# Linear attention values brought back to rows by transposes, in a bank of their own

## The chip, the cores and the metric

The kernel runs on one core of one Trainium2 chip. The metric is device time in microseconds (us) of one execution. Names of engines: PE is TensorE, DVE is VectorE, ACT is ScalarE, POOL is GpSimd, SP is SyncE.

## The reference

One transformer block on x of 4 batches x 1024 tokens x 256 channels. The output is x plus an attention part plus a mixture-of-experts part, both of the layer-normed x. The change is in the attention part, whose core is

```
sq, sk = elu(q)+1, elu(k)+1                      # 16 heads of 16 channels
# causal linear attention, chunk by chunk, S and z carried along
num = einsum(scores*mask, v) + einsum(sq, S);  den = scores.sum + einsum(sq, z)
local  = num / clip(den, EPS)
# memory of 4 banks per head: fine outputs weighted by w, and a coarse one (banks summed)
w      = softmax(mean over tokens of n_f)        # one weight per bank, head and batch
memory = exp_prob*out_fine + (1-exp_prob)*out_coarse
output = (gate*memory + (1-gate)*local) @ w_o.T
```

## The kernel before

Three phases follow one another: tokens, experts, and attention, which takes about the second half of the time. Only `attention_phase` and the list that orders it, `attention_order`, are touched.

The attention phase walks over 4 batches x 8 tiles of 128 tokens, 32 tiles in all. One list, `ATT_ORDER`, names the steps; every engine walks the same list and does the steps that are its own, in that order, so a step that waits on an engine holds back all that stands behind it on that engine. Engines meet by semaphores (`since(engine, signal, count)` waits). Nothing is planned by cost.

PE writes into a ring of 7 PSUM banks (`a_ring`). Every step that needs a bank takes the next one in the order of the list, and first waits (`use_bank`) until the step that had it 7 uses before has been read. The banks of a tile are taken in this order: four for `scores`, then `outT`, `coarseT`, `keys`, one projection for later tiles (`keys_side`: a q, k or v step), `oproj`, `hidden`, four for `norms`, zero to three further projection steps or `xT` steps, two for `values`, `gate`, `local`. So the projection of `keys_side` takes the bank of the first `scores` step, and waits for DVE's first `probs` product of the tile.

The steps which the change and the prediction touch, per tile t (0 to 7) of batch b:

- `scores` (PE L1417, DVE L1681): products of keys and queries into four banks. DVE multiplies each by the causal mask into `probs`, four products of 256 columns.
- `values` (PE L1452, ACT L1574): `probs` times v, transposed: 32 partitions per head, of which 17 (16 values and the denominator, `HE`) are used. ACT copies them to `valT`.
- `local` (PE L1463 and L1474, DVE L1687 to L1690): PE adds up, in one bank, the state's part (`sq` times `state`, L1463) and the tile's own values, brought back from `valT` to rows of tokens by matmuls with the picked columns of an identity (L1474, four matmuls of 68 columns, which the trace shows as eight passes). DVE then makes `den`, its reciprocal, and one product of 256 columns into `local`, which is a part of `mem_rows`.
- `state` and `fold` (PE L1497, DVE L1712): the two halves of a tile are added to the running state in the bank `a_sums`, and DVE copies it out under a mask of heads, 272 columns.
- `mean`, `mexp`, `weights`: once in a batch, at t = 0, the softmax over the memory banks: DVE L1644 to L1648, ACT's exponential L1526, DVE L1654 to L1661.
- `norms` (PE L1398, ACT L1554, DVE L1669 to L1674), `coef`, `rest`, `fine`, `oproj`: the memory part and the output projection, partly one or two tiles late. POOL adds up the `fine` products (L1769 to L1774).
- `rows` on ACT (L1533) scales the gathered expert rows for POOL.

The tile's end in the list is, in the kernel before:

```
order += ahead + [("values", b, t, 0), ("values", b, t, 1)] + behind + [("gate", b, t, 0)]
...
order.append(("local", b, t, 0))
```

## Time and profile before

| | |
|---|---|
| three runs | 708.75, 712.3, 714.91 us (median 712.3) |
| the profiled execution | 708.62 us, span 706.7 us |
| busy in the span | PE 89%, DVE 72%, ACT 50%, POOL 44% |
| busy in 465 to 475 us, an ordinary stretch of attention | PE 10.00, DVE 8.44, ACT 5.40, POOL 6.25 of 10 us |

The profiled execution takes 1.9 us more than its span. It lies at the lower end of the runs, 3.7 us under the median. In attention PE is shown busy almost without a break and DVE nearly so; an engine's busy time counts a matmul up to its modelled end, so PE at 10 of 10 us is not PE at its peak.

### The profile page before, as it was taken

The page shows a single profiled execution, that of the slowest core. Times are in us where ns is not written, and L with a number is a line of the kernel's source. Part 1 is how long each engine was busy: PE and PEld are TensorE (multiplying, and loading weights), DVE is VectorE, ACT ScalarE, POOL GpSimd, SP SyncE. Part 2 cuts the span into 40 slices and gives each one's busy share as a digit, 9 for nine tenths or more (in the row PEclk, how much of TensorE's full clock was granted, in tenths as well). Part 3 has the DMA queues.
Part 4 walks back from the last instruction along what each step waited for, and adds up shares of the span by engine and source line. Part 5 has one row for each costly group of instructions (what it writes and reads, how often), then busy time and mean ns, then how long its engine had stood idle before and what let it go on. Part 6 is the DMA issues. An engine that isn't in the chain of part 4 may idle for free. (4 is left out here: it accounts for less than half of the span.)

```text
span 706.7 us, 22451 instructions
## 1 busy us (share of the span) xinstructions
PE 626.9 (89%) x7874; PEld 520.5 (74%) x7874; DVE 509.9 (72%) x1362; ACT 355.9 (50%) x902; POOL 313.4 (44%) x406
## 2 busy tenths in 40 slices
PE   1997869699499999999968999989998999989885
PEld 0785748578399999999956777777776777777663
DVE  3674829358466666666656988889888788888886
ACT  4453625252434444444435766556565475646542
POOL 1153543707481000000030766656675566666775
PEclk9999989989599999999978999999999999999996
DMA  8128271534353333333350012221140202103120
GB/s 283 64 91 277 78 257 56 189 136 149 121 167 116 117 120 118 121 114 117 116 183 34 18 33 92 84 85 32 36 137 29 84 25 65 60 17 92 33 63 32
DMA packets 60123, 71.39 MB, mean 101 GB/s; under 512 B 7612, under 2 KB 55068, under 8 KB 60028
## 3 DMA queue, kind: packets, MB, share of 16 engines
q1 hardware_dynamic: 50956, 52.61, 22.9%
q0 software_dynamic: 6656, 16.86, 7.3%
q8 instruction: 67, 1.10, 0.7%
q10 hardware_dynamic: 2416, 0.59, 0.4%
q14 instruction: 28, 0.23, 0.1%
HBM read 38.45 MB, written 31.59 MB: 99 GB/s over the span
## 5 line engine op out<-in xcount | busy, mean ns | idle before, releaser
L1741 POOL TENSOR_TENSOR tick_a<-lane 128x1 f32<-128x1 f32 x32 | 6.3, 196 | 148.1 <-POOLq L834 145.8
L1744 POOL DMA_INDIRECT yg<-d_grouped_y,from_row x64 | 62.5, 977 | 15.5 <-issue 11.6
L978 ACT ACTIVATE hb<-e_h 88x256 fp32r<-88x256 f32 x72 | 27.5, 382 | 52.7 <-PE e_h L953 52.7
L87 PE MATMUL e_up<-wb,xb 128*128 x144 | 53.0, 368 | 0.5 <-issue 0.5
L1554 ACT ACTIVATE with_mem<-a_ring 128x340 f32<-128x340 f32 x128 | 47.0, 450 | 7.8 <-PE a_ring L1398 7.5
L1010 DVE TENSOR_TENSOR h_sb<-e_up,silu 128x176 f32<-128x176 f32 x72 | 24.6, 342 | 35.3 <-ACT silu L973 35.3
L87 PE MATMUL e_y<-wd,hb 88*128 x146 | 48.7, 334 | 1.0 <-DVE hb L1017 1.0
L1769 POOL TENSOR_TENSOR mem_rows<-mem_rows 128x512 f32<-128x512 f32 x16 | 24.3, 1518 | 54.5 <-DVE mem_rows L1721 54.5
L1681 DVE TENSOR_TENSOR probs<-a_ring,causal 128x256 f32<-128x256 f32 x128 | 45.1, 415 | 3.5 <-remote 3.3
L89 PE MATMUL e_up<-wb,xb 128*128 x144 | 46.9, 326 | 0.0
L88 PE MATMUL e_up<-wb,xb 128*128 x144 | 46.9, 326 | 0.0
L973 ACT ACTIVATE silu<-e_up 128x176 f32<-128x176 f32 x72 | 22.9, 318 | 41.1 <-PE e_up L89 41.1
L1474 PE MATMUL a_ring<-ident,valT 128*128 128x68 f32 x256 | 35.3, 279 | 8.4 <-ACT valT L1574 8.4
L88 PE MATMUL e_y<-wd,hb 88*128 x146 | 41.6, 285 | 0.0
L1474 PEld LDWEIGHTS a_ring<-ident,valT 128*128 128x128 f32 x256 | 31.0, 191 | 14.2 <-issue 11.0
L89 PE MATMUL e_y<-wd,hb 88*128 x146 | 41.3, 283 | 0.0
L1017 DVE TENSOR_TENSOR hb<-e_h,hb 88x256 fp32r<-88x256 f32 x72 | 30.3, 420 | 14.7 <-ACT hb L978 12.5
L821 POOL DMA_INDIRECT d_rows<-v,slot_i x32 | 34.0, 1063 | 9.5 <-issue 9.5
L821 POOL DMA_INDIRECT d_rows<-sqT,slot_i x32 | 33.0, 1032 | 9.5 <-issue 9.5
L1430 PE MATMUL a_ring<-wo,attT 128*128 128x256 f32 x128 | 35.2, 399 | 1.3 <-ACT attT L1563 1.1
L1571 ACT ACTIVATE hid<-a_ring,b 64x128 f32<-64x128 f32 x32 | 11.6, 364 | 48.6 <-PE a_ring L1440 36.8
L87 PE MATMUL t_g<-xT,shared_w 128*128 128x512 f32 (+1 forms) x48 | 22.1, 461 | 15.6 <-issue 15.6
(300 smaller groups left out, 2069.7 us busy)
## 6 DMA issues: line engine op xcount, KB each, us to landing
xg<-d_rows SPq DMA_DIRECT2D x77, 128.0 KB, 2.0
d_grouped_y<-y_sb SPq DMA_DIRECT2D x73, 128.0 KB, 1.8
d_base<-xn_in SPq DMA_DIRECT2D x8, 512.0 KB
xn_in<-d_xn SPq DMA_DIRECT2D x4, 1024.0 KB
total<-d_base SPq DMA_DIRECT2D x8, 512.0 KB
out<-total SPq DMA_DIRECT2D x7, 512.0 KB, 3.3
mem_rows<-in_w_up SPq DMA_DIRECT2D x4, 704.0 KB
v<-in_x_tok SPq DMA_DIRECT2D x2, 1024.0 KB
```

Of the source, the lines that this page charges most:

```text
L87: pe.matmul(out, a[0], b[0], start=start, stop=False)
L88: pe.matmul(out, a[0], b[1], start=False, stop=False)
L89: return pe.matmul(out, a[1], b[0], start=False, stop=stop)
L821: pool.indirect_dma_start(d["rows"], bass.IndirectOffsetOnAxis(ap=slot_i[u][:, k, t:t + 1], axis=0), xn[u][:, t, :], None).then_inc(s_sc[u ...
L978: act.activation(hb[o][0][:, :, :], ps_h[o][0:FC, 0:2 * P].rearrange("p (k n) -> p k n", k=2), ACT.Copy).then_inc(s_hh, 1)
L1010: dve.tensor_tensor(h_sb[q][:, :], ps_up[q][:, F:2 * F], silu[q][:, :], ALU.mult).then_inc(s_h, 1)
L1017: dve.tensor_tensor(hb[o][1][:, :, :], ps_h[o][0:FC, 0:2 * P].rearrange("p (k n) -> p k n", k=2), hb[o][0][:, :, :].bitcast(F32), ALU.subt ...
L1430: mm = pe.matmul(ps[:, 0:H], attT[t % 2][:, m, :], c["wo"][:, m, :], start=(m == 0), stop=(m == KC - 1))
L1474: mm = pe.matmul(ps[:, 0:NH * HE].rearrange("p (m g n) -> p m g n", m=KC, g=PP)[:, :, g, :], valT[:, g, :], pick.rearrange("p (m r) e -> p ...
L1554: act.activation(with_mem[((b - 1) * NT + t) % 3][:, j:NP:PP, :], ps[:, 0:KC * WN].rearrange("p (m w) -> p m w", m=KC), ACT.Copy).then_inc ...
L1681: dve.tensor_tensor(probs[:, j, :, :], ps[:, 0:4 * CH].rearrange("p (h i) -> p h i", i=CH), c["causal"][:, 0:CH].unsqueeze(1).broadcast_to ...
L1744: pool.indirect_dma_start(yg[tile % GATHERS][:, k, :], None, d["grouped_y"], bass.IndirectOffsetOnAxis(ap=c["from"][:, k, tile:tile + 1], ...
```

## The change

1. `local` on PE is only the state's part, in a bank of its own, the heads in another order (by_group). ACT copies it to `so_far` (272 columns).
2. A new step `picks`: PE transposes `valT` by four transposes of 128x128 into another bank. DVE adds `so_far` to it into `heads` (272 columns; in the first tile of a batch, half of the partitions are copied and half are added), and makes `den`, reciprocal and product from `heads`; the product is two of 128 columns, since the heads are in another order.
3. The exponential `mexp` on ACT comes after `gate` instead of ahead of `values`, and DVE's `weights` in the next tile, behind the `scores` products, instead of ahead of the second `fold`.

```
@@ attention_order
+        if t == 1:
+            order.append(("weights", b, 0, 0))
         if i:
             order += [("coef", *tiles[i - 1], 0), ("rest", *tiles[i - 1], 0)]
...
         if t == 0:
-            order += [("mean", b, 0, 0), ("mexp", b, 0, 0)]
+            order.append(("mean", b, 0, 0))
         order += ahead + [("values", b, t, 0), ("values", b, t, 1)] + behind + [("gate", b, t, 0)]
+        if t == 0:
+            order.append(("mexp", b, 0, 0))
...
-        if t == 0:
-            order.append(("weights", b, 0, 0))
...
-        order.append(("local", b, t, 0))
+        order += [("local", b, t, 0), ("picks", b, t, 0)]
@@ PE, local
+                        by_group = ps[:, 0:NH * HE].rearrange("p (g m n) -> p m g n", g=PP, m=KC)
...
-                               state[(2 * t + h) % 3][:, m, :],
-                               start=(first and m == 0), stop=last, skip_group_check=last)
+                               state[(2 * t + h) % 3][:, m, :].rearrange("p (g n) -> p g n", g=PP),
+                               start=(m == 0), stop=True, skip_group_check=True)
+                    elif what == "picks":
                         since(pe, s_valT, b * 2 * NT + 2 * (t + 1))
                         for g in range(4):
-                            mm = pe.matmul(ps[:, 0:NH * HE].rearrange("p (m g n) -> p m g n", m=KC, g=PP)[:, :, g, :],
-                                           valT[:, g, :], pick.rearrange("p (m r) e -> p m r e", m=KC),
-                                           start=(t == 0 and g == 0), stop=(g == 3))
+                            mm = pe.transpose(ps[:, g * P:(g + 1) * P], valT[:, g, :], c["ident"][:, :])
@@ ACT
+                    elif what == "local":
+                        since(act, s_both, b * NT + t)
+                        of = slice(0 if t else CH, P)
+                        act.activation(so_far[of, :, :], ps[of, 0:NH * HE].rearrange("p (h e) -> p h e", e=HE),
+                                       ACT.Copy).then_inc(s_before, 1)
@@ DVE
-                        link(dve.scalar_tensor_tensor(den[:, :], heads[:, :, HD], EPS, over_keep[:, :],
-                                                      ALU.max, ALU.mult))
+                        since(dve, s_before, b * NT + t + 1)
+                        since(dve, ready["picks"], b * NT + t + 1)
+                        if t:
+                            link(dve.tensor_tensor(heads[:, :, :], inside, so_far[:, :, :], ALU.add))
+                        else:
+                            dve.tensor_copy(heads[0:CH, :, :], inside[0:CH])
+                            link(dve.tensor_tensor(heads[CH:P, :, :], inside[CH:P], so_far[CH:P, :, :], ALU.add))
+                        dve.sem_inc(s_both, 1)
+                        link(dve.scalar_tensor_tensor(den[:, :], heads[:, :, HD], EPS, over_keep[:, :], ALU.max, ALU.mult))
                         link(dve.reciprocal(den[:, :], den[:, :]))
-                        dve.tensor_tensor(local[:, :].rearrange("p (h e) -> p h e", e=HD), heads[:, :, 0:HD],
-                                          den[:, :].unsqueeze(2).broadcast_to([P, NH, HD]),
-                                          ALU.mult).then_inc(s_local, 1)
+                        for m in range(KC):
+                            ins = dve.tensor_tensor(
+                                local[:, m * P:(m + 1) * P].rearrange("p (g r e) -> p g r e", g=PP, r=2),
+...
+                        ins.then_inc(s_local, 1)
```

The order of PE's instructions around the step, for tile 3 of a batch. Before, from the state's part on:

```order
L1463 MATMUL a_ring<-state,sqT 64x136
L1474 MATMUL a_ring<-ident,valT 128x2x34 [waits a_valT]
L1474 MATMUL a_ring<-ident,valT 128x2x34 x3
...
L1406 MATMUL a_ring<-ident,skT 128x128 [waits a_sk,a_local]
L1406 MATMUL a_ring<-ident,skT 128x128
L87 MATMUL a_ring<-a_xT,wqkv 128x512 [waits a_xl,a_probs]
```

and with the change:

```order
L1470 MATMUL a_ring<-state,sqT 64x4x34
L1477 MATMUL a_ring<-ident,valT 128x128 [waits a_valT,a_with]
L1477 MATMUL a_ring<-ident,valT 128x128 x3
...
L1410 MATMUL a_ring<-ident,skT 128x128 [waits a_sk,a_both]
L1410 MATMUL a_ring<-ident,skT 128x128
L87 MATMUL a_ring<-a_xT,wqkv 128x512 [waits a_xl,a_probs]
```

The transposes stand where the matmuls stood, `keys` (the transposes of skT) now waits for DVE's addition and no longer for its product, and the projection behind it (L87) still waits for `probs`. On DVE, the end of the first tile of a batch and the beginning of the second, before:

```order
L1648 TENSOR_TENSOR mw<-mw,mw_m 128x64 [waits a_dve]
L1654 TENSOR_REDUCE mw_m<-mw 128x16 [waits a_mexp]
L1655 RECIPROCAL mw_m<-mw_m 128x16 [waits a_dve]
L1656 TENSOR_TENSOR mw_m<-mw_m,half_gate 128x16 [waits a_dve]
L1658 TENSOR_TENSOR mw<-mw,mw_m 128x64 [waits a_dve]
L1661 TENSOR_TENSOR mw<-mw,alive 128x64 [waits a_dve]
L1712 TENSOR_TENSOR state<-a_sums,same_head 128x272 [waits a_ps_state,a_dve]
L1687 SCALAR_TENSOR_TENSOR den<-a_ring,over_keep 128x16 [waits a_ps_local]
L1689 RECIPROCAL den<-den 128x16 [waits a_dve]
L1690 TENSOR_TENSOR mem_rows<-a_ring,den 128x256 [waits a_dve]
L1681 TENSOR_TENSOR probs<-a_ring,causal 128x256 [waits a_ps_values,a_ps_scores] x4
```

and with the change:

```order
L1655 TENSOR_TENSOR mw<-mw,mw_m 128x64 [waits a_dve]
L1730 TENSOR_TENSOR state<-a_sums,same_head 128x272 [waits a_ps_state]
L1699 COPY heads<-a_ring 64x272 [waits a_ps_picks,a_before]
L1700 TENSOR_TENSOR heads<-a_ring,so_far 64x272
L1702 SCALAR_TENSOR_TENSOR den<-heads,over_keep 128x16 [waits a_dve]
L1703 RECIPROCAL den<-den 128x16 [waits a_dve]
L1705 TENSOR_TENSOR mem_rows<-heads,den 128x128 [waits a_dve]
L1705 TENSOR_TENSOR mem_rows<-heads,den 128x128
L1689 TENSOR_TENSOR probs<-a_ring,causal 128x256 [waits a_ps_values,a_ps_scores] x4
L1662 TENSOR_REDUCE mw_m<-mw 128x16 [waits a_mexp]
L1663 RECIPROCAL mw_m<-mw_m 128x16 [waits a_dve]
```

The five instructions of `weights` have moved from ahead of the second `fold` to behind the four `probs` products, and what stands between `fold` and `probs` has grown from three instructions to six (five in the other tiles). On ACT, at the end of the same tile, before:

```order
L1526 ACTIVATE mw<-mw 128x64 [waits a_mx]
L1574 ACTIVATE valT<-a_ring 128x4x64 [waits a_ps_local,a_ps_values] x2
L1550 ACTIVATE v<-a_ring 128x16x16 [waits a_ps_v]
L1578 ACTIVATE e_t<-a_ring,half_b 128x1 [waits a_rest,a_ps_gate]
L1533 ACTIVATE yg<-yg,cw 128x256 [waits a_ga1]
```

and with the change:

```order
L1573 ACTIVATE valT<-a_ring 128x4x64 [waits a_ps_picks,a_ps_values] x2
L1549 ACTIVATE v<-a_ring 128x16x16 [waits a_ps_v]
L1582 ACTIVATE e_t<-a_ring,half_b 128x1 [waits a_rest,a_ps_gate]
L1525 ACTIVATE mw<-mw 128x64 [waits a_mx]
L1578 ACTIVATE so_far<-a_ring 64x272 [waits a_both,a_ps_local]
L1532 ACTIVATE yg<-yg,cw 128x256 [waits a_ga1]
```

The copies to `valT` no longer stand behind the exponential; the new copy `so_far` does.

## Rows read from the trace of the kernel before

**Rows 1.** The page: busy time of the engines, and the chain that ended last.

```profile
PE 626.9 (89%) x7874; PEld 520.5 (74%) x7874; DVE 509.9 (72%) x1362; ACT 355.9 (50%) x902; POOL 313.4 (44%) x406
...
PE 28%; DVE 9%; issue 4%; POOL 3%; ACT 3%; another core or an unknown queue 1%; ACTq 0%; POOLq 0%; DVEq 0%
```

**Rows 2.** Waits, 375 to 706 us: waiter, waited for, us, times, longest.

```profile
DVE den L1687 <- PE a_ring L1474: 9.6, 13, 1.1
...
DVE total L1729 <- PE a_ring L1430: 4.5, 12, 1.4
DVE state L1712 <- PE a_sums L1497: 4.2, 12, 0.5
...
DVE den L1687 <- PE a_ring L1463: 2.7, 4, 0.7
```

**Rows 3.** Timeline of an ordinary tile: start, duration, instruction [idle before].

```profile
412.81 1.11 PE L1474 MATMUL a_ring<-ident,valT 128*128 128x68 f32 x8
412.82 0.62 ACT L1547 ACTIVATE sqT<-a_ring 128x512 f32<-128x512 f32 x1
...
413.85 0.69 PE L1417 MATMUL a_ring<-masked,skT 32*64 32x128 f32 x32
413.95 0.17 DVE L1687 SCALAR_TENSOR_TENSOR den<-a_ring,over_keep 128x16 f32<-128x16 f32 x1 [0.71 <-PE a_ring L1474]
...
414.47 0.44 PE L1426 MATMUL a_ring<-ident,att 128*128 128x128 f32 x2
...
414.79 1.41 DVE L1681 TENSOR_TENSOR probs<-a_ring,causal 128x256 f32<-128x256 f32 x4
...
414.96 0.41 PE L1406 MATMUL a_ring<-ident,skT 128*128 128x128 f32 x2
...
415.26 0.50 PE L87 MATMUL a_ring<-a_xT,wqkv 128*128 128x512 f32 x1
...
422.92 1.11 PE L1474 MATMUL a_ring<-ident,valT 128*128 128x68 f32 x8
...
423.67 0.43 DVE L1712 TENSOR_TENSOR state<-a_sums,same_head 128x272 f32<-128x272 f32 x1
...
424.07 0.17 DVE L1687 SCALAR_TENSOR_TENSOR den<-a_ring,over_keep 128x16 f32<-128x16 f32 x1
```

**Rows 4.** Groups of instructions, 375 to 706 us: busy us, mean ns | idle before.

```profile
L1712 DVE TENSOR_TENSOR state<-a_sums,same_head 128x272 f32<-128x272 f32 x60 | 26.2, 437 | 6.3 <-PE a_sums L1497 4.2 <-DVE skT L1629 1.5 <-remote 0.3
...
L1690 DVE TENSOR_TENSOR mem_rows<-a_ring,den 128x256 f32<-128x256 f32 x32 | 13.6, 425 | 1.1
...
L1648 DVE TENSOR_TENSOR mw<-mw,mw_m 128x64 f32<-128x64 f32 x4 | 0.9, 234 | 0.1
...
L1560 ACT ACTIVATE k_tok<-a_ring 128x256 f32<-128x256 f32 x32 | 12.5, 391 | 1.4 <-PE a_ring L1406 1.0 <-issue 0.2
```

**Rows 5.** Timeline, a fold behind a wait and a semaphore increment on DVE.

```profile
511.75 0.44 DVE L1712 TENSOR_TENSOR state<-a_sums,same_head 128x272 f32<-128x272 f32 x1 [0.21 <-DVE skT L1629]
```

**Rows 6.** Timeline of a batch's first tile, 463 to 467 us.

```profile
463.14 0.24 DVE L1648 TENSOR_TENSOR mw<-mw,mw_m 128x64 f32<-128x64 f32 x1
...
463.41 0.26 ACT L1526 ACTIVATE mw<-mw 128x64 f32<-128x64 f32 x1 [2.47 <-DVE mw L1648]
...
463.70 0.22 DVE L1654 TENSOR_REDUCE mw_m<-mw 128x16 f32<-128x64 f32 x1 [0.32 <-ACT mw L1526]
...
464.36 1.08 PE L1474 MATMUL a_ring<-ident,valT 128*128 128x68 f32 x8 [1.82 <-ACT valT L1574]
...
464.97 0.44 DVE L1712 TENSOR_TENSOR state<-a_sums,same_head 128x272 f32<-128x272 f32 x1
...
466.08 0.17 DVE L1687 SCALAR_TENSOR_TENSOR den<-a_ring,over_keep 128x16 f32<-128x16 f32 x1 [0.67 <-PE a_ring L1463]
...
466.92 0.41 DVE L1681 TENSOR_TENSOR probs<-a_ring,causal 128x256 f32<-128x256 f32 x1
```

**Rows 7.** The stretch behind a first tile in batches 2 and 3: busy us, clock (PEclk).

```profile
466.08:476.21 10.13, 10.13 (x196) 7.77 (x204) 8.41 (x22) 6.18 (x17) 6.36 (x8) 1.00 0.40 123
548.90:560.34 11.44, 11.44 (x196) 9.00 (x204) 8.25 (x21) 6.40 (x17) 6.34 (x8) 0.86 0.32 105
```

**Rows 8.** Timeline near the end of the last batch, DVE.

```profile
678.75 0.43 DVE L1712 TENSOR_TENSOR state<-a_sums,same_head 128x272 f32<-128x272 f32 x1
679.11 0.17 DVE L1687 SCALAR_TENSOR_TENSOR den<-a_ring,over_keep 128x16 f32<-128x16 f32 x1
```

More of the change, by code:

```diff
@@ L1520, in walk @@
                         continue
-                    if what not in ("xT", "q", "k", "v", "keys", "outT", "coarseT", "hidden", "values", "gate",
+                    if what not in ("xT", "q", "k", "v", "keys", "local", "outT", "coarseT", "hidden", "values", "gate",
                                     "mexp", "norms", "rows"):
@@ L1608, in walk @@
                     what, bb, t = what.removesuffix(".dve"), b, n
-                    if what in ("mexp", "v", "coarseT", "keys", "hidden", "outT", "values", "gate", "mask", "rows"):
+                    if what in ("mexp", "v", "coarseT", "keys", "hidden", "outT", "values", "gate", "mask", "rows",
+                                "local"):
                         continue
```

37 lines of the change are left out of this document (20 added, 17 removed).

## The prediction

> **What bounds the kernel now.** I read the page first, then the waits of the attention half, then the timeline of one ordinary tile, and last the first tile of a batch, which is the one that looks different. The page shows PE as the busiest engine and as the largest part of the chain that ended last [rows 1]. By it alone, a shorter step on PE would shorten the kernel. The waits speak against so simple a reading: in attention DVE waits for the values brought back by PE only 9.6 us in 13 of 32 tiles, and in the 4 first tiles of the batches 2.7 us for the state's part that comes last there [rows 2]. In the other 15 tiles DVE comes to `den` without waiting at all, as at 424.07 us, right behind the fold that began at 423.67, and at 679.11 us in the last batch [rows 3, 8]. There DVE is as late as PE is.
>
> The timeline of the tile shows why both are tight. From the first of the value matmuls (412.81) PE goes on to `scores` at 413.85 and to the projection L87 at 415.26, which is 2.45 us [rows 3]. That projection takes the bank of the first `scores` step, so by the kernel's ring it waits for DVE's first `probs` product (its wait on a_probs in the order). DVE begins `den` at 413.95 and `probs` at 414.79; the first of the four products lasts as long as another of 256 columns, 0.42 us [rows 3, 4], so it ends at 415.21. PE starts the projection 0.05 us later. The loop to be watched is therefore: values back, DVE's chain up to the first `probs`, projection, the rest of PE's tile (7.66 us until 422.92), values back. PE's own work takes just as long beside it. A gain on PE counts only if DVE's chain doesn't grow by more.
>
> **The change, part by part.**
>
> *PE's transposes.* Before, the matmuls hold PE for 1.04 us (412.81 to 413.85) in eight passes. Transposes of the same size run in `outT`, `coarseT` and `keys`: four of them start between 414.47 and 414.96, 0.49 us [rows 3]. With the gap of about 0.15 us that a wait ahead of `scores` may leave uncovered, since a shorter step covers less of it (an estimate), PE gains 0.40 us in a tile, from 0.55 down to 0.25 us if that gap is larger. In 32 tiles this would be 13 us, if PE alone set the time.
>
> A page of the Trainium skill (TensorE: Matmul & The Clock Gate, Terms) has the transpose mode four times faster for fp32. By it the step would take 0.26 us and PE would gain 0.63 us in a tile; the rows give 0.49 us for four. Neither changes the sum below, in which PE waits anyway.
>
> *DVE's chain.* Before: `den` to `probs`, 0.84 us (413.95 to 414.79, and 466.08 to 466.92) [rows 3, 6]. After, step by step. The addition of 272 columns from a bank and SBUF is priced by the fold of the same size, 0.44 us, and 0.04 us to the next linked instruction (the distance left between such instructions in the three of the chain). A semaphore increment and a wait behind it stand in one place of the trace, where 0.21 us pass instead of 0.04 [rows 5]; I take 0.10 us, between nothing and 0.17. Then `den` 0.17 and 0.04, the reciprocal 0.25 and 0.04. Then two products of 128 columns: 64 columns take 0.234 us and 256 take 0.425 [rows 4], so 128 take 0.30; unlinked instructions begin about 0.08 us before the one ahead has ended (`probs` begins 0.35 us behind a product of 0.42), so 0.22 us each. Sum 0.58 + 0.50 + 0.43 = 1.51 us, **0.67 us more in a tile**. The lower bound has no price for the increment and 0.18 us for each product, 0.45 us more; the upper has 0.17 us and products that don't overlap, 0.91 us more. Nothing hides it: the chain stands in the loop ahead of `probs`, and behind it on DVE are queued `probs`, `coef`, `rest`, the addition of `oproj` and the folds, for which PE, POOL and the ring wait.
>
> *Where it counts.* In the 15 tiles in which DVE doesn't wait now, all of the 0.67 us goes into the loop, since what DVE does between `probs` and the second fold is tied to PE by waits that move with it: 15 x 0.67 = 10.1 us.
>
> In the 13 tiles with a wait, mean 0.74 us [rows 2], the wait goes and something else comes late. Transposes that take 0.49 us instead of 1.04 are ready some 0.7 us behind their start. But DVE also needs `so_far`. Its copy stands on ACT behind the two activations of a q or k projection: the second starts at 412.82 with 0.62 us, the next may start about 0.47 us behind it, and a copy of its size takes 0.39 to 0.41 us [rows 3, 4]: 0.9 us behind the start of the picks. So from picks to projection it is 0.7 or 0.9, plus 1.51, 0.42 and 0.05: 2.7 or 2.9 us, where it was 2.45. That is 0.25 us more in tile 5 of three batches, where a v projection stands there, and 0.45 in tiles 3 and 7: 3 x 0.25 + 6 x 0.45 = 3.5 us. Behind the copy on ACT is queued the scaling of the gathered rows for POOL, 0.4 us later, which has slack.
>
> The remaining four waits are those of the second tiles, which also get `weights`: five instructions from 463.70 to 464.97, 1.27 us [rows 6], which now stand on DVE ahead of `coef`. 0.67 - 0.74 + 1.27, less a wait of 0.18 us for `oproj` that they cover, is 1.0 us, 4.1 us in four batches.
>
> *The first tiles.* Here the change does what the trace asks for. ACT stands 2.47 us in front of the exponential, the values wait behind it, and PE waits 1.82 us for `valT` [rows 6]. After the change PE has state's part and transposes done before DVE is there. DVE ends the mean's subtraction at 463.38, folds by 463.74, and then waits for `so_far`, which stands behind the exponential (to 463.67) and takes 0.4 us more: 463.98. Copy of one half 0.27 us, then 1.51: `probs` at 465.76 instead of 466.92, 1.16 us earlier. Four times 4.6 us. So the 1.82 us of PE's wait don't come back whole; what is late next is DVE's mean and then the copy on ACT.
>
> *The clock.* In one of four batches the wait of the first tile was followed by a stretch at a granted clock of 0.86, between its two levels of 1.2 and 2.4 GHz, which took 11.44 us where the same stretch at 1.00 took 10.13 [rows 7]. PE now waits less there: 1.3 us gained.
>
> **Sum**: 10.1 + 3.5 + 4.1 - 4.6 - 1.3 = +11.8 us. The profiled execution of 708.6 us would become 720.4. It lies 3.7 us under the median of the runs, so against 712.3 us it is **724 us**. The bounds of the chain, 0.22 us less and 0.24 more in the 24 tiles or so in which it counts, make this 719 to 730.
>
> **Rivals.**
>
> 1. *DVE's waits absorb the work, no change.* If the ring's wait on `probs` weren't binding (PE could run its 0.40 us ahead), DVE would work without waits: 32 x 0.67 = 21.4 us against 9.6 + 2.7 of waits for values, 4.2 for the state, some 3 of 4.5 for `oproj` outside the last tiles [rows 2], and 1.3 us for the exponential (4 x 0.32 [rows 6]) and 1.3 of clock: 21.4 - 22.1, near zero, 712 us; with other prices of the chain 705 to 719. For it: DVE has these waits. Against: 0.05 us between `probs` and the projection, and the row of the order that says what the projection waits for.
>
> 2. *PE sets the time, faster.* If the chain costs little beside PE, 0.40 x 28 = 11.2, and (1.82 + 0.4) x 4 = 8.9, and 1.3 of clock: 21 us less, 691 us. For it: the page, with PE 28% of the chain and DVE 9% [rows 1]. Against: the 15 tiles without a wait of DVE.
>
> 3. *ACT and the clock, slower still.* If `so_far` is late in every tile, through ACT's queue or late signals of the state's part, and not in nine, 0.2 to 0.5 us more in 20 tiles is added: 728 to 735 us. It decides from the point at which the copy ends later than DVE's second fold. The clock belongs here: PE would now wait some 0.6 us in each tile ahead of the projection. At 1.3 us for a stretch, as in rows 7, in 28 tiles it would be 36 us more, 760 us. The trace speaks against it: three of four waits of 1.8 us had no such sequel. The Trainium skill (TensorE: Matmul & The Clock Gate, Part 4) says that transposes don't count as PE being busy for the clock, which would make this case likelier, as four matmuls in a tile become transposes. No row here shows transposes alone; the 1.00 in rows 7 stands over a stretch with six transposes among its 196 matmul passes.
>
> 4. *The transposes don't run in one pass.* Then PE gains nothing; as it waits anyway, only tile 5 and the like get 0.4 us later: about 726 us, inside the range.
>
> **How the numbers follow.** My case has 0.52, rival 1 0.24, rival 2 0.14, rival 3 0.08 (0.02 of it the clock), rival 4 0.02. A measurement here tells about 1% from no change, that is 7.1 us: 705.2 to 719.4. Slower by more: nearly all of my case, and rivals 3 and 4 and a tail of rival 1, 0.60. Within: most of rival 1 and the low end of mine, 0.25. Faster: rival 2 and a little of rival 1, 0.15. The range that should hold 8 in 10 takes in my case, rival 1 and the lower part of rival 3: 705 to 731 us. It leaves out rival 2, which has 0.14, and the far end of rival 3.
>
> **What would show it.** In the trace after: DVE from its addition (L1697) to `probs` (L1689) 1.4 to 1.6 us; DVE's waits for picks nearly gone, but waits for ACT's `so_far` in tiles 3 and 7; PE's idle time ahead of the projection L87 0.4 to 0.7 us in most tiles, released by `probs`; PE's start of picks to start of `scores` 0.5 to 0.8 us; the wait of 1.82 us in the first tiles gone; tiles of the last batch 0.6 us longer each. I am wrong if the projection starts without waiting for `probs`, or if DVE's unlinked instructions overlap so far that the chain grows by under 0.4 us; then it is rival 1 or 2. A granted clock under 1.00 in ordinary tiles would be rival 3.

## The result, and the profile after

The changed kernel is slower. The first comparison gave 730.2 us median (726.87 to 734.51, 4 runs) against 711.22 (708.75 to 714.91, 4 runs), a ratio of 1.027 with an interval of 1.019 to 1.034. A second comparison on another occasion gave 739.72 against 714.81 us, 1.035 (1.027 to 1.044). Ratios and 714.81 leave out the runs in the chip's slower state, which occurred only on that occasion (with them its median for the kernel before is 716.24). The forecast was 724 us and 705 to 731. The profiled execution took 734.51 us with a span of 732.7, where my sum led to 720.4. It is the slowest of its four runs and that of the kernel before the fastest, so the two profiles lie 25.9 us apart where the medians lie 19.0.

The page of the changed kernel, busy time and the chain that ended last, beside [rows 1]:

```profile
PE 619.0 (84%) x7746; PEld 507.4 (69%) x7746; DVE 534.3 (73%) x1431; ACT 367.8 (50%) x934; POOL 314.7 (43%) x406
...
PE 25%; DVE 15%; issue 6%; ACT 4%; another core or an unknown queue 1%; DVEq 0%; POOL 0%; ACTq 0%; POOLq 0%
```

PE does 7.9 us less and DVE 24.4 us more, and DVE's part of the chain grows from 9% to 15%. The work went from the engine that looks busier to the one on which the tile waits.

The waits of attention in the changed kernel, 375 to 733 us (waiter, waited for, us, times, longest), beside [rows 2]:

```profile
PE a_ring L87 <- DVE probs L1689: 21.5, 23, 1.6
...
PE a_ring L1421 <- DVE a_xT L1623: 6.4, 6, 1.7
DVE heads L1697 <- PE a_ring L1477: 6.2, 3, 2.7
...
DVE total L1747 <- PE a_ring L1434: 5.8, 12, 1.4
...
DVE heads L1697 <- ACT so_far L1578: 5.6, 6, 1.1
...
PE a_ring L1434 <- DVE probs L1689: 5.0, 5, 1.2
...
PE a_ring L1421 <- ACT sqT L1546: 2.9, 6, 0.6
PE a_ring L1421 <- ACT skT L1546: 2.0, 6, 0.3
```

The first row is the loop of the prediction: PE now stands 0.93 us in front of the projection in 23 tiles, until DVE's first `probs` is there. In five tiles of the last batch the output projection waits for the same thing, 5.0 us. DVE's wait for PE's values is down from 13 times to 3, and it waits for ACT's `so_far` in 6 tiles, as forecast. Two things were not forecast. The 3 waits that are left are long, up to 2.7 us. And PE waits 11.3 us in 18 places ahead of `scores` (L1421), for the readers of the projections of the tile before, where the kernel before had 2.3 us in 3.

The timeline of an ordinary tile, where [rows 3] stood (start, duration, instruction, idle before):

```profile
503.83 0.44 DVE L1697 TENSOR_TENSOR heads<-a_ring,so_far 128x272 f32<-128x272 f32 x1 [0.78 <-ACT so_far L1578]
...
504.42 0.18 DVE L1702 SCALAR_TENSOR_TENSOR den<-heads,over_keep 128x16 f32<-128x16 f32 x1 [0.15 <-DVE heads L1697]
...
504.63 0.25 DVE L1703 RECIPROCAL den<-den 128x16 f32<-128x16 f32 x1
504.73 0.73 POOL L1776 TENSOR_TENSOR yg<-yg 128x256 f32<-128x256 f32 x1 [1.44 <-ACT yg L1532]
...
504.92 0.88 DVE L1705 TENSOR_TENSOR mem_rows<-heads,den 128x128 f32<-128x128 f32 x2
...
505.53 0.85 POOL L1777 TENSOR_TENSOR total<-total,yg 128x256 f32<-128x256 f32 x1
...
505.73 1.40 DVE L1689 TENSOR_TENSOR probs<-a_ring,causal 128x256 f32<-128x256 f32 x4
...
506.19 0.50 PE L87 MATMUL a_ring<-a_xT,wqkv 128*128 128x512 f32 x1 [0.73 <-DVE probs L1689]
```

From the addition to `probs` pass 1.90 us; it was to be 1.51. Up to `den` the sum holds to 0.01 us: 0.59 against 0.58. What is long are the two products, 0.88 us together. The first begins while POOL adds `yg`, and `probs` begins 0.27 us after POOL has ended at 505.46, as if only then the product could run. Over all tiles the addition's part is 0.58 to 0.60 us, and `den` to `probs` is 1.27 us in the mean and 0.97 to 1.53, where it was 0.84 in 30 of 31 tiles.

The lengths of the two instructions over the run (x count: min, median, max in ns):

```profile
L1702 DVE SCALAR_TENSOR_TENSOR den<-heads,over_keep x32: 178/182/875, 380.4 to 722.9; 128x16 f32<-128x16 f32 x32
```

```profile
L1705 DVE TENSOR_TENSOR mem_rows<-heads,den x64: 276/287/679, 380.9 to 724.6; 128x128 f32<-128x128 f32 x64
```

The same instruction takes 0.28 us or 0.68, and `den` 0.18 or 0.88. Their means are 276 and 415 ns. The kernel before had 175 ns for `den`, never over 176, and 424 to 426 ns for the product of 256 columns.

All 29 products over 0.30 us and all 13 `den` over 0.20 us began while POOL was adding or multiplying. Of the 54 short ones none did, but for three `den` that began within 2 ns of POOL. Each long product ended 0.15 us after the end of the instruction of POOL that it met, and each long `den` 0.03 us after it: in the tile above, 504.92 + 0.68 = 505.60 against 505.46. So the instruction is not slowed in proportion; it ends a fixed time after POOL's.

PE has a new kind of pause. In tile 5 of batches 1, 2 and 3 it stops inside the eight matmuls of the state's part, ahead of the last 2, 4 and 6 of them, for nothing that the profile shows:

```profile
435.59 0.39 PE L1470 MATMUL a_ring<-state,sqT 128*64 128x136 f32 x2 [0.73 <-issue]
...
525.43 0.62 PE L1470 MATMUL a_ring<-state,sqT 128*64 128x136 f32 x4 [1.01 <-issue]
...
616.70 0.68 PE L1470 MATMUL a_ring<-state,sqT 128*64 128x136 f32 x6 [0.93 <-issue]
```

DVE's three long waits for the picks follow them (at 436.68, 527.10 and 618.08). The kernel before has no such pause there.

An ordinary tile takes 11.0 us where it took 10.1, and a tile of the last batch 9.6 us where it took 8.8.

### The profile page after: what moved, and what is told of

It reads as the page before. It is cut to its first block, busy times and chain, and to the rows that moved or that the text cites. A ratio compares the mean times of both kernels' runs of the same rounds, so it can differ in the third digit from the quotient of the medians.

```text
span 732.7 us, 22426 instructions
## 1 busy us (share of the span) xinstructions
PE 619.0 (84%) x7746; PEld 507.4 (69%) x7746; DVE 534.3 (73%) x1431; ACT 367.8 (50%) x934; POOL 314.7 (43%) x406
## 4 chain that ended last, share of the span: by engine, by line
PE 25%; DVE 15%; issue 6%; ACT 4%; another core or an unknown queue 1%; DVEq 0%; POOL 0%; ACTq 0%; POOLq 0%
PE a_ring L1434 4%; PE a_ring L87 3%; PE a_ring L1444 3%; PE a_ring L1402 3%; PE a_ring L1456 2%; PE a_ring L88 2%; PE a_ring L89 2%; DVE probs L1689 2%; DVE heads L1697 1%; DVE mem_rows L1705 1%; PE a_sums L1496 1%; DVE den L1702 1%; PE a_ring L1374 1%; DVE rn L1679 1%; DVE den L1703 1%
## 5 line engine op out<-in xcount | busy, mean ns | idle before, releaser
L87 PE MATMUL e_up<-wb,xb 128*128 x144 | 53.4, 371 | 0.5 <-issue 0.5
L1787 POOL TENSOR_TENSOR mem_rows<-mem_rows 128x512 f32<-128x512 f32 x16 | 24.4, 1523 | 61.3 <-DVE mem_rows L1739 61.3
L87 PE MATMUL e_y<-wd,hb 88*128 x146 | 48.6, 333 | 1.0 <-DVE hb L1017 1.0
L1434 PE MATMUL a_ring<-wo,attT 128*128 128x256 f32 x128 | 38.0, 424 | 6.1 <-DVE probs L1689 5.0
L1017 DVE TENSOR_TENSOR hb<-e_h,hb 88x256 fp32r<-88x256 f32 x72 | 30.3, 421 | 14.7 <-ACT hb L978 12.5
L1787 POOL TENSOR_TENSOR prod<-prod 128x512 f32<-128x512 f32 x16 | 21.6, 1352 | 41.5 <-DVE prod L1739 41.5
L904 PE MATMUL e_x<-ident,xg 128*128 128x128 f32 x148 | 29.0, 278 | 7.0 <-DMA xg<-d_rows 7.0
L87 PE MATMUL t_y<-shared_w,hT 128*128 128x256 f32 (+1 forms) x96 | 28.6, 298 | 7.2 <-DVE hT L688 6.8
```

What stands on the lines that cost most here:

```text
L87: pe.matmul(out, a[0], b[0], start=start, stop=False)
L904: mm = pe.transpose(ps_x[q][:, kc * P:(kc + 1) * P], xg[j_buf][:, kc * P:(kc + 1) * P], c["ident"][:, :])
L1017: dve.tensor_tensor(hb[o][1][:, :, :], ps_h[o][0:FC, 0:2 * P].rearrange("p (k n) -> p k n", k=2), hb[o][0][:, :, :].bitcast(F32), ALU.subt ...
L1434: mm = pe.matmul(ps[:, 0:H], attT[t % 2][:, m, :], c["wo"][:, m, :], start=(m == 0), stop=(m == KC - 1))
L1787: link(pool.tensor_tensor(part[:, :, :, :], prod[:, :, 0:2, :], prod[:, :, 2:4, :], ALU.add))
```

## The experiments

Eleven runs were made on three occasions, which the table names; the first two rows are the comparison of the result. The kernel before took 718, 683 and 716 us on them, so I compare by the ratio to it, or within one occasion. For a comparison across occasions I use a length that leaves out the phases ahead of attention: from `den` in the second tile of batch 1 to the end of the last instruction that isn't an issue of a transfer, both read from the timeline of the one profiled execution.

Both measures have a weakness. The two profiles of the changed kernel differ by 2.6 us in length, those of the kernel with the exponential alone by nothing. And the kernel before was profiled only once, 311.5 us. Its medians, less 3.8 us of time outside that length and its mean start in the kernels beside it, give some 322, 312 and 314 us on the three occasions (an estimate). So the kernel before was some 10 us longer on the first occasion, and the ratios of the first four runs are up to 1.4% too favourable to them.

| kernel | us (ratio, interval) | that length, us |
|---|---|---|
| before | 711.2 | 311.5 |
| changed | 730.2 (1.027, 1.019 to 1.034) | 339.9 |
| changed, again (third occasion) | 739.7 (1.035, 1.027 to 1.044) | 342.5 |
| sum kept in PSUM (first) | 724.0 (1.011, 1.003 to 1.019) | 326.2 |
| transposes only (first) | 746.7 (1.040, 1.032 to 1.048) | 350.0 |
| exponential only (first) | 700.4 (0.976, 0.968 to 0.984) | 304.6 |
| exponential only, again (third) | 703.8 (0.986, 0.982 to 0.990) | 304.6 |
| without the addition (first) | 704.2 (0.981, 0.974 to 0.989) | 311.5 |
| without so_far too (second) | 666.8 (0.975, 0.973 to 0.977) | 297.1 |
| without POOL's rows (second) | 692.6 (1.012, 1.010 to 1.014) | 323.0 |
| 8 transposes ahead (second) | 710.1 (one run) | 335.9 |
| 64 transposes ahead (second) | 711.7 (1.042, 1.037 to 1.047) | 330.8 |
| exponential, and a dummy addition (third) | 713.8 (1.000, 0.996 to 1.005) | 315.1 |

**The sum kept in PSUM.** The edit to the changed kernel:

```
-                            link(dve.tensor_tensor(heads[:, :, :], inside, so_far[:, :, :], ALU.add))
+                        of = slice(0 if t else CH, P)
+                        link(dve.tensor_tensor(inside[of], inside[of], so_far[of, :, :], ALU.add))
...      den and the products read inside (the bank) in place of heads (SBUF),
...      and the bank of the picks is free after the product, no longer after the addition
```

> The changed kernel, but DVE writes the sum of picks and so_far back into the bank of the picks instead of into heads, so that den and the two products read one operand from PSUM and one from SBUF (in the first tile of a batch only the upper half is added, nothing is copied). The same is computed. Theory A (den and the products are stretched because both operands lie in SBUF and POOL adds at the same time): the chain from the addition to probs falls from 1.87 to about 1.45 us, den and products stand at their medians (0.17, 0.28) without stretches, and the kernel is 8 to 10 us faster than the changed one, about 1.013 of the kernel before. Theory B (the products are long for their access pattern or for being two instead of one): the chain stays within 0.1 us of 1.87, the time at 1.025 of the kernel before.

It took 1.011 of the kernel before, and the length fell by 13.7 us between the profiles (9 to 13 us by the medians, an estimate made as above). From the addition to `probs` pass 1.51 us in the mean, where it was 1.86. The products and `den` in it:

```profile
L1702 DVE TENSOR_TENSOR mem_rows<-a_ring,den x64: 280/287/292, 383.6 to 713.2; 128x128 f32<-128x128 f32 x64
```

```profile
L1699 DVE SCALAR_TENSOR_TENSOR den<-a_ring,over_keep x32: 174/175/176, 383.1 to 712.5; 128x16 f32<-128x16 f32 x32
```

The medians are about those of the changed kernel (287 and 175 ns, for 287 and 182), and the tails are gone: 292 and 176 ns at most, though 54 of the 64 products began while POOL was adding or multiplying. The access pattern and the split in two products are the same in both, so theory B falls. That both operands lie in SBUF is what makes them long.

Not all of the 13.7 us need be the chain. An ordinary tile takes 10.61 us in place of 11.02, but PE's three pauses in tile 5 are gone too, though PE has the same 7746 matmuls in the same order. The PSUM bank is also held longer. PE's wait has moved with it from the projection to `keys`, which now needs DVE's product:

```profile
PE a_ring L1410 <- DVE mem_rows L1702: 13.6, 26, 0.9
```

In ordinary tiles the projection still starts 0.05 us after the end of the first `probs`.

**The changed kernel without POOL's rows.** The two additions of gathered rows are left out, and with them the experts' part of the output:

```
-                        link(pool.tensor_tensor(rows[:, 0, :], rows[:, 0, :], rows[:, 1, :], ALU.add))
-                        pool.tensor_tensor(total[:, t, :], total[:, t, :], rows[:, 0, :], ALU.add).then_inc(s_ysum, 1)
+                        pool.sem_inc(s_ysum, 1)
```

> The changed kernel without POOL's two additions of the gathered expert rows (yg and total); the experts' part is left out of the output. POOL keeps its three additions per tile for the memory part. Theory A (these two additions run beside den and the products and stretch them, since both sides read from SBUF): no product over 0.30 us and no den over 0.20 in ordinary tiles, the chain from the addition to probs 1.45 to 1.5 us, and 8 to 12 us less than the changed kernel, 1.010 to 1.015 of the kernel before. Theory B (the stretches come from something else, such as ACT writing or the gathers' transfers): products still up to 0.68 us, time within 3 us of the changed kernel.

The ratio is 1.012, as expected. It took 19.1 us less than the kernel with 64 transposes, which was measured beside it but also pays for these at the start; by length it is 7.8 us under that kernel and 17 to 20 us under the changed one. From the addition to `probs` pass 1.50 us in most tiles, as expected too. DVE's two products together, from the first's start to the second's end, take 0.49 us in 28 of 32 tiles. In the changed kernel they took 0.49 us in 3 tiles and 0.61 to 0.88 in all the others.

```profile
L1705 DVE TENSOR_TENSOR mem_rows<-heads,den x64: 276/291/600, 358.6 to 685.3; 128x128 f32<-128x128 f32 x64
```

With both operands still in SBUF the stretch is gone where POOL's two additions are gone. Four products over 0.30 us and six `den` over 0.20 remain, up to 0.60 and 0.88 us, so the expectation of none was too clean. The longest of each ran beside what POOL still does for the memory part. Why the length fell by more than the 8 to 12 us expected is not shown.

**The exponential and weights alone.** The kernel before, with `mexp` behind `gate` and `weights` in the next tile:

```
+        if t == 1:
+            order.append(("weights", b, 0, 0))
...
-            order += [("mean", b, 0, 0), ("mexp", b, 0, 0)]
+            order.append(("mean", b, 0, 0))
...
+        if t == 0:
+            order.append(("mexp", b, 0, 0))
...
-        if t == 0:
-            order.append(("weights", b, 0, 0))
```

> The kernel before with only the exponential and the weights moved as in the change; the values come back by matmuls as before. Theory: the wait of 1.8 us in the four first tiles shrinks to under 0.7, about 1.2 us each; the weights cost the second tiles about 0.5 us each, since DVE has a wait of 0.74 there that takes part of them: 3 us less in all, 0.995 of the kernel before (0.990 to 1.000). Rival (DVE's mean and fold end only just ahead of the values, so nothing is gained in the first tiles and the weights cost): 1.003.

> The kernel before with only the exponential and the weights moved, once more, with more rounds, as the best version so far. Theory: 8 us less by the waits of the first tiles and second tiles, as in its first profile, and up to 9 more where the kernel before has a stretch of lower clock behind these waits in more than one batch: 0.976 to 0.989 of the kernel before. If the clock has no part in it: 0.986 to 0.990.

It is faster than the kernel before both times, 0.976 and 0.986 with more runs; the first ratio is one of those that flatter. The gain is larger than the theory's 3 us. From `den` in a first tile back to the one ahead of it, 12.05 us became 10.17: 1.88 us in each batch and not 1.2. Before and after, `den` in the tile ahead (the other ends are `den` at 466.08 [rows 6] and 462.55):

```profile
454.03 0.17 DVE L1687 SCALAR_TENSOR_TENSOR den<-a_ring,over_keep 128x16 f32<-128x16 f32 x1 [1.05 <-PE a_ring L1474]
```

```profile
452.38 0.17 DVE L1690 SCALAR_TENSOR_TENSOR den<-a_ring,over_keep 128x16 f32<-128x16 f32 x1 [1.05 <-PE a_ring L1476]
```

And the second tiles, which now hold the 1.27 us of `weights`, did not grow: 10.10 us against 10.13. The kernel before has three waits of DVE in that tile, 0.18 us for `oproj`, 0.41 for `with_mem` and 0.83 for the values; with `weights` there, none of them stands in the timeline. I had counted only the first and the last against the added time, and 0.74 for the last.

**The transposes alone.** The changed kernel with `mexp` and `weights` at their old places:

```
-            order.append(("mean", b, 0, 0))
+            order += [("mean", b, 0, 0), ("mexp", b, 0, 0)]
...      and weights again ahead of the second fold of tile 0
```

> The changed kernel with the exponential and the weights where they stood before, so that only the way back of the values is changed. Theory of my sum (the move gains 1.2 us in each of four first tiles and loses 1.1 us in each of four second tiles, where the weights stand in DVE's chain): within 3 us of the changed kernel, 1.022 to 1.030 of the kernel before. Rival (the long waits of the first tiles also cost clock in every batch): 5 us or more slower than the changed kernel, over 1.033.

1.040 of the kernel before, and 10.1 us more in length than the changed kernel: the rival was right. The stretch behind a first tile in this kernel, in the changed one and in the one with the exponential alone (us, PE busy, PEld, DVE, ACT, POOL, granted clock):

```profile
473.72:486.62 12.90, 10.71 (x180) 7.69 (x180) 9.45 (x24) 6.34 (x18) 6.77 (x8) 0.87 0.35 103
```

```profile
471.35:482.29 10.94, 9.37 (x178) 6.91 (x180) 10.19 (x28) 6.56 (x18) 7.01 (x8) 1.00 0.24 74
```

```profile
462.55:472.65 10.10, 10.10 (x196) 7.76 (x204) 9.54 (x26) 6.28 (x18) 6.56 (x8) 1.00 0.28 89
```

In this kernel the granted clock is 0.87 behind each of the three later first tiles, and the stretch takes 12.9 us instead of 10.9. In the kernel before only one of three had that [rows 7]. In the kernel with the transposes the move is thus worth 1.2 us ahead of the first tile (12.77 against 11.56 us from one `den` to the next) and 2.0 us behind it, in each batch.

**The addition left out.** DVE reads the picks in their bank; the state's part is left out of the output:

```
-                            link(dve.tensor_tensor(heads[:, :, :], inside, so_far[:, :, :], ALU.add))
                         dve.sem_inc(s_both, 1)
...      den and the products read inside in place of heads
```

> The changed kernel without DVE's addition: den and the products read the picks in their bank, and the part of the state is left out of the output. PE's and ACT's work is all there. Theory (a tile lasts as long as DVE's chain ahead of the projection lets it, and PE's shorter step is worth 0.4 us once that chain is short): the chain is 0.85 to 0.95 us, tiles take 9.7 to 10.0 us, the kernel is 0.980 to 0.990 of the kernel before. Rival (PE gains nothing by the transposes, whose wait for valT or slower passes take it back): tiles stay at 10.1 us or more, 0.995 or over.

The ratio fits the theory (0.981), but it owes that to the kernel before, which was slow on that occasion (some 322 us by the estimate above); by length, 311.5 us, the kernel is no faster than the profile of before. The reason doesn't fit either: ordinary tiles took 10.13 us, as with matmuls, and those of the last batch 8.78, as before. The length is 6.9 us over that of the exponential alone, whose PE work per tile is longer. By itself, then, the way back by transposes with ACT's copy cost something, even with DVE's chain as short as before.

**so_far left out too.** Neither ACT's copy nor DVE's wait for it:

```
-                        act.activation(so_far[of, :, :], ps[of, 0:NH * HE].rearrange("p (h e) -> p h e", e=HE),
-                                       ACT.Copy).then_inc(s_before, 1)
+                        act.sem_inc(s_before, 1)
...
-                        since(dve, s_before, b * NT + t + 1)
```

> As the kernel without the addition, and ACT's copy to so_far and DVE's wait for it left out too (the state's part is left out of the output). Theory (the 5.3 us by which the kernel without the addition was longer than the one with only the exponential moved come from so_far being late in ten tiles, 6.1 us, and from three pauses of PE in tile 5): 3 to 5 us less than without the addition, 0.972 to 0.978 of the kernel before; ordinary tiles stay at 10.1 us, since DVE's own work fills them. If PE's shorter step were worth its 0.4 us in every tile once nothing waits on so_far: ordinary tiles 9.7 us and 0.965 or less.

The ratio, 0.975, lies in what was expected; the length fell by 14.4 us, to 297.1, and not by 3 to 5. That is 7.5 us under the exponential alone. It is the most that PE's shorter step can be worth here, since ACT's copy of some 0.4 us in a tile is gone as well, and it is uneven: three tiles of each batch take 9.4 to 9.7 us and those of the last batch 8.45, but some four tiles of each batch still take 10.1 to 10.3. My expectation that ordinary tiles would stay at 10.1 is refuted, and so is 9.7 in all. Where it doesn't arrive, PE stands ahead of `scores`:

```profile
PE a_ring L1421 <- DVE a_xT L1621: 5.2, 6, 1.0
...
PE a_ring L1421 <- ACT sqT L1546: 3.1, 6, 0.6
...
PE a_ring L1421 <- ACT skT L1546: 2.2, 6, 0.4
```

`scores` needs the banks of the projections ahead of the values. PE's 1.04 us of matmuls had covered the time in which ACT and DVE read them. Shorter picks uncover it: the kernel before has 2.3 us of such waits, this one 10.5.

**A dummy addition.** The kernel with the exponential alone, and one more instruction on DVE; PE and ACT unchanged:

```
+                        link(dve.tensor_tensor(extra[:, :, :], heads,
+                                               c["ident"][:, 0:HE].unsqueeze(1).broadcast_to([P, NH, HE]), ALU.add))
                         link(dve.scalar_tensor_tensor(den[:, :], heads[:, :, HD], EPS, over_keep[:, :],
```

> The kernel before with the exponential and the weights moved, and one more instruction on DVE ahead of den: an addition of 272 columns from the bank and SBUF whose result nobody reads. PE and ACT are as before. Theory (DVE's chain ahead of the projection sets the tile): a tile grows by 0.48 us in the 22 or so tiles where DVE comes to den without a wait, by less in the 9 with a wait of 0.7 us; 11 to 14 us more than without it. Rival (the waits of DVE and PE that move along take it up): under 5 us more.

10 to 11 us more by the medians of the same occasion and 10.5 in length: a little under the 11 to 14 expected, and twice what the rival allowed. An ordinary tile takes 10.58 us against 10.10: the 0.48 us of one addition, whole. Its waits, and those of the kernel without it:

```profile
DVE extra L1691 <- PE a_ring L1477: 7.1, 9, 1.1
...
DVE extra L1691 <- PE a_ring L1466: 2.1, 4, 0.6
```

```profile
DVE den L1690 <- PE a_ring L1476: 6.7, 9, 1.1
...
DVE den L1690 <- PE a_ring L1465: 2.1, 4, 0.6
```

This speaks against rival 1 more plainly than any other run. DVE's waits for the values don't take up the work. They are still there, 9 times 0.8 us, and the whole loop with PE has grown longer. PE's idle time in this kernel doesn't stand ahead of the projection, as the prediction had it, but one step earlier, ahead of `keys`, which waits for DVE's product:

```profile
PE a_ring L1409 <- DVE mem_rows L1696: 11.1, 30, 0.9
```

When the two `keys` transposes are through, the first `probs` is there too, and the projection starts 0.05 us behind it, as in the kernel before. So the loop closes through `keys` as much as through the ring; both ends hang on the same chain of DVE. Only in the last batch does the addition cost less, 0.10 us in a tile (8.87 against 8.77).

**Where PE's pauses stand.** Transposes whose results are overwritten, once, at the start of attention (8, and in a second kernel 64):

```
                         since(pe, s_x, bb * 16 + 16)
+                        if (b, n, j) == (1, 1, 0):
+                            for _ in range(8):
+                                pe.transpose(ps[:, 0:P], c["ident"][:, :], c["ident"][:, :])
```

> The changed kernel with 8 transposes more on PE, once, right at the start of attention, whose results are overwritten. They move every later instruction of PE by 8 matmuls with their weight loads. In the changed kernel PE pauses 0.7 to 1.0 us in tile 5 of batches 1, 2 and 3, after 2, 4 and 6 of the eight matmuls of the state's part (L1470), waiting for nothing that the profile shows; the same places show it in the runs with the transposes alone and without the addition. Theory (PE's next piece of instructions comes late: the place is fixed in the instruction stream): the pauses move by 8 matmuls, to 6, 4 and 2 matmuls ahead of the state's part, inside the step before it (L1496), of about the same length; the whole time changes by under 2 us. Rival (a transfer or a semaphore of the tile makes PE wait): the pauses stay at L1470 after 2, 4 and 6.

I had read the rows the wrong way round: the count stands behind the pause, so it comes ahead of the last 2, 4 and 6 of eight. Eight instructions more ahead of it should then put it ahead of the last 2, 4 and 6 of the sixteen matmuls of the step before. Measured:

```profile
415.19 0.21 PE L1499 MATMUL a_sums<-v,k_tok 64*32 64x34 f32 x1 [1.34 <-issue]
...
507.13 0.25 PE L1499 MATMUL a_sums<-v,k_tok 64*32 64x34 f32 x3 [1.34 <-issue]
...
596.48 0.26 PE L1499 MATMUL a_sums<-v,k_tok 64*32 64x34 f32 x5 [1.07 <-issue]
```

Ahead of the last 1, 3 and 5: moved by 7 matmuls, with the same step of 2 from batch to batch, and longer, 1.1 to 1.3 us. The length is 4.0 us under the changed kernel's first profile, where under 2 was expected. A semaphore or a transfer that belongs to the tile would not move with instructions put in at the start of attention. The second run of the changed kernel has the pauses at the old places again (0.73, 1.04 and 0.93 us).

> As the kernel with 8 transposes more, but with 64 (once, at the start of attention, 3 to 4 us of PE by themselves at most, of which PE may have some free). Theory of late instructions: none of the three pauses stands in tile 5 behind the values any more, nor the waits of DVE for the picks of 1.6 to 2.7 us and the stretches of lower clock that follow; 4 to 7 us come back in attention, less what the 64 cost; a pause may turn up in another tile, where the border now falls behind the values. Rival: the three pauses stay.

With 64 the three are gone, and the tile that had them takes 10.31, 10.65 and 10.30 us in place of 11.41, 12.27 and 12.08: 4.5 us back. One pause of 0.88 us turned up in another tile (606.16 us), and two tiles with a stretch of lower clock are longer than in the changed kernel, 13.6 us for 12.9 and 12.4 for 11.3. The length is 9 to 12 us under the changed kernel's two. The timed ratio, 1.042, shows no gain against 1.027 and 1.035, but the 64 transposes are in it, and no unshifted changed kernel was measured on that occasion. So it is shown that the place of the pauses moves with the instructions; what they cost in the end is not.

The place alone doesn't make a pause. The kernels with the sum in PSUM and without `so_far` have the changed kernel's matmuls of PE in the same order and no such pause: the longest idle time of PE without a visible cause is 0.47 us in the one and under 0.28 in the other. What PE must have done ahead of the place for it to pause stays open.

**The changed kernel again.**

> The changed kernel once more, beside the next two, since the phases ahead of attention differ in length from one call to the next (the kernel before took 711, 718 and 683 us in three calls). If attention costs the same number of microseconds each time, this is 19 to 30 us over the kernel before, 1.027 to 1.043 of it. Below 1.02 would mean that the first comparison overstated the change.

1.035, 24.9 us. The first comparison didn't overstate the change. It lies 5.9 us under this one, and why is not shown.

## Why the prediction was right in sign and short in size

The forecast was 724 us, with 705 to 731 as the range, and the time was 730.2, which is 0.8 us inside it. The second comparison, with 24.9 us more than the kernel before where 11.8 were forecast, would lie outside. So the sign comes out of the reasoning, but that the range held is in part luck.

*The loop held.* Values, DVE's chain, projection: in 23 tiles the projection waits for `probs`, the dummy addition costs its 0.48 us in full in an ordinary tile, and the kernel is slower. The direction came out of the 0.05 us between `probs` and the projection in [rows 3], and of the tiles in which DVE doesn't wait. Rival 1 and rival 2 fell with it. I had overlooked the second way round, from DVE's product to `keys`.

*The term of DVE's chain was mis-sized.* I put 0.67 us in a tile, bounds 0.45 to 0.91 (by the prices named there the lower bound is 0.50). It was 1.02 in the mean, 0.59 us up to `den`, as I had it, and 1.27 behind it for 0.93. The step that failed is "64 columns take 0.234 us and 256 take 0.425, so 128 take 0.30". The 0.425 was measured on a product that read PSUM and SBUF, and the new ones read SBUF twice while POOL adds. Alone they take 0.287 us, as I said; beside POOL up to 0.68. Keeping the sum in PSUM, which the computation allows, brings 13.7 us of length back (PE's pauses, absent there, may be a part of it), and taking POOL's two additions away brings most of the pairs to 0.49 us. The Trainium skill (SBUF — State Buffer, section SBUF: two separate sides) says that DVE and GpSimd share a pair of ports as a lock, held for a whole instruction, and that a DVE instruction with two SBUF inputs needs it against a GpSimd instruction that reads SBUF. The rows agree: 0.88 us for a pair beside POOL, 0.49 with PSUM or without POOL's additions, and ends of the long ones that follow POOL's by 0.15 and 0.03 us. The rule would have warned me. So would a row of the trace of before that I hadn't read, an instruction of DVE that reads SBUF only and whose length varies sixfold:

```profile
L1669 DVE TENSOR_SCALAR rn<-with_mem x32: 201/852/1247, 367.2 to 685.9; 128x80 f32<-128x80 f32 x32
```

*Where it counts.* The forecast had 0.67 us more in the tiles without a wait, 0.45 in tiles 3 and 7 and 0.25 in tile 5. Measured from `probs` in one tile to `probs` in the next, tile 4 grew by 0.86 to 0.87 and tile 3 by 0.84 to 0.88 us: the waits of DVE took up nothing in either kind. The kernel with the sum in PSUM has the chain of the forecast (1.51 us), and there most of these tiles grew by 0.50 us and those of the last batch by about 0.7. So this part of the sum was sound for the chain that it was made for.

*Late so_far.* The copy was late in tiles 3 and 7, as forecast, by 0.66 to 1.13 us, 5.6 us in six waits. From picks to projection these tiles take 3.3 and 3.6 us, where I had 2.9. The run without `so_far` shows that its whole weight may be larger: 14.4 us of length, of which the pauses of PE (absent there) and ACT's own time are a part. How these divide stays open.

*PE's gain.* From the picks' start to the start of `scores` PE needs 0.59 us where nothing waits, in place of 1.04; I had 0.64. But 9.0 us of the 12.8 that I reckoned come back as waits ahead of `scores`. I had written that PE "waits anyway", and had not looked at what the shorter step uncovers in the ring.

*The first and second tiles.* In the changed kernel the first tiles became 0.65 us shorter by the same measure (0.90 in the one with the clock), where 1.16 was forecast, and the second ones 0.87 longer in batches 2 and 4, where 1.0 was forecast (batch 3 had the stretch of lower clock before, batch 1 follows the experts). With the sum in PSUM the first tiles gain 1.31, so what is missing there is the longer chain again. The move alone measures 8.5 us by the span (706.7 to 698.2), 6.9 by length and 1.4% by the longer comparison, 10 us. Its length is accounted for: three times 1.88 us in first tiles and the 1.3 us of clock. The 1.27 us of weights cost nothing there, since three waits of 1.42 us together take them up; I had counted two of them. The clock was taken from one profile in which one wait of 1.8 us in three had a sequel; in the kernel with the transposes alone all three had one, behind waits of 1.2 us.

*Not foreseen:* the three pauses of PE in tile 5. The kernel with 64 transposes, where they are absent, has 4.5 us less in these tiles than the changed one.

*The sum.* By length, in steps: exponential -6.9 us, transposes and copy with no addition +6.9, the addition in PSUM +14.7, its result in SBUF +13.7: +28.4. My +11.8 had the third nearly whole, and lacked the fourth. These are differences of single profiles, and the one of the kernel before is a fast one: by the medians the change costs 19 to 25 us.

*Rival 3* was right in a part. Granted clocks of 0.86 to 0.88 stand behind the pauses (527.69 to 539.92 us and 448.49 to 459.80) and behind `den` in the second tile of batch 1 (0.87), and one of 0.68 in a tile of the last batch. Against the same tile of another batch they cost 0.1 to 1.8 us, some 4 us together. In ordinary tiles the clock is otherwise 1.00, with PE waiting 0.7 to 1.0 us in each, and though four of their matmuls have become transposes; that side of rival 3 finds no support here.

Of the versions that compute everything, the best is the kernel with the exponential and weights moved and nothing else: 0.986 of the kernel before (0.982 to 0.990). It beats both.

## What to carry to other kernels

Before work is moved off the busiest engine, find the loop: an instruction that starts 0.05 us behind another engine's result is a link in it, and a dummy instruction in one engine's chain tells in one run whether waits would take the work up. Price a DVE instruction for the place where its operands lie, and for what POOL does in that moment; a result that may stay in PSUM should stay there. And a change of two parts is worth trying in its parts: here one half gains 7 to 10 us and the other costs about 30.

## What the runs showed of the hardware

- A DVE instruction on 128 columns with both operands in SBUF took 0.28 us alone and up to 0.68 beside POOL's additions; one on 16 columns 0.18 and up to 0.88. With one operand in PSUM the longest of 64 and of 32 were 0.292 and 0.176 us. The long ones ended 0.15 us (128 columns, 29 of 29) and 0.03 us (16 columns, 13 of 13) after the instruction of POOL that was running when they began.
- PE paused 0.7 to 1.3 us at the same places of its instruction stream in the two runs of the changed kernel. Eight matmuls put in ahead moved them by seven. In these three runs an instruction transfer of 16 KB begins 2.2 to 2.6 us before each of the nine pauses ends. That PE ran out of instructions is the reading that fits; it was not isolated, and two kernels with the same matmuls in the same order had no such pause.
- Behind a first tile the clock was granted at 0.87 over 12.9 us in three of three places of one kernel, after waits of PE of 1.2 us, and at 1.00 in two of three of another, after waits of 1.8 us.
- Four fp32 transposes of 128x128 let the next matmul start 0.59 us behind them; the eight passes of 68 columns took 1.04 us.
